# Loads of x and turned x issued from GpSimd's queue instead of SyncE's

## The reference

```
q = rotary(x @ Wq + bq)           16 heads of 32
k = rotary(x @ Wk + bk)           one head, shared by all 16
v = x @ Wv + bv                   one head, shared
attn = softmax(q k^T / sqrt(32))
x = layernorm(x + (attn v) @ Wo + bo)
W1, W2, W3 = clip(round(w / mean|w|), -1, 1)
x = layernorm(x + (sigmoid(x W1^T) * (x W2^T)) @ W3^T)      inner width 1408
```

## Time and profile before

| | us |
|---|---|
| median of 3 runs | 601.56 (600.76 to 603.36) |
| the profiled execution | 602.12 |
| its span | 600.3 |
| busy PE / DVE / ACT / POOL | 547.1 / 472.5 / 426.1 / 300.6 |
| granted share of TensorE's clock, mean | 0.971 |

### The profile page before, as it was taken

How to read it: one execution, slowest core, us unless ns; L and a number is a source line. 1 busy time by engine, 2 the same in 40 slices (tenths; PEclk the granted TensorE clock), 3 DMA queues, 4 the chain that set the end, 5 groups by cost and what they waited for, 6 DMA issues and landing times.

```text
span 600.3 us, 9190 instructions
## 1 busy us (share of the span) xinstructions
PE 547.1 (91%) x2984; PEld 273.1 (45%) x2984; DVE 472.5 (79%) x635; ACT 426.1 (71%) x865; POOL 300.6 (50%) x398
## 2 busy tenths in 40 slices
PE   9778989899788999999799999999599999989993
PEld 5444545444443444454344445354344444444441
DVE  3867878979888999899989899889989897444433
ACT  2697867779967988787878898687979796233300
POOL 2219696939589734788346325896553300201011
PEclk9789999999898999999999999999799999999997
DMA  8680428239999897999999988989899989000001
GB/s 310 190 304 17 127 50 302 55 75 195 208 193 162 151 177 150 177 198 199 220 206 185 168 162 153 183 187 197 170 208 178 169 177 192 36 1 36 1 0 70
DMA packets 217119, 92.12 MB, mean 153 GB/s; under 512 B 204400, under 2 KB 205552, under 8 KB 216560
## 3 DMA queue, kind: packets, MB, share of 16 engines
q1 hardware_dynamic: 209952, 77.61, 62.5%
q0 software_dynamic: 6144, 12.60, 10.1%
q10 hardware_dynamic: 976, 1.33, 0.6%
HBM read 20.20 MB, written 4.19 MB: 41 GB/s over the span
## 4 chain that ended last, share of the span: by engine, by line
PE 66%; DVE 10%; ACT 8%; issue 7%; POOL 4%; DMA 3%; SPq 1%; POOLq 0%; ACTq 0%; DVEq 0%
PE a_ps L1300 13%; PE b_ps L1300 7%; PE s_ps L1345 6%; PE s_ps L1313 6%; PE e_ps L1300 5%; PE c_ps L1403 5%; PE b_ps L1313 4%; PE a_ps L1231 3%; DVE p_all L1048 3%; PE c_ps L1385 3%; PE a_ps L1313 2%; ACT p_all L749 2%; PE b_ps L1285 2%; DMA pt_sb<-p_all 2%; PE s_ps L1356 2%
## 5 line engine op out<-in xcount | busy, mean ns | idle before, releaser
L749 ACT ACTIVATE p_all<-s_ps,sh_sb 128x512 f32<-128x512 f32 x192 | 130.1, 683 | 54.3 <-DVE sh_sb L1041 53.7
L1048 DVE SCALAR_TENSOR_TENSOR p_all<-p_all 128x1024 f16<-128x1024 f32 x96 | 133.0, 1385 | 4.6 <-ACT p_all L757 4.5
L1041 DVE TENSOR_REDUCE sh_sb<-s_ps 128x2 f32<-128x1024 f32 x96 | 116.5, 1214 | 17.0 <-PE s_ps L1345 17.0
L757 ACT ACTIVATE p_all<-p_all 128x1024 f16<-128x1024 f32 x96 | 101.7, 1059 | 2.0
L1300 PE MATMUL a_ps<-late,q 128*128 128x512 f16 x352 | 84.9, 385 | 4.9 <-ACT th L720 3.2
L1345 PE MATMUL s_ps<-k_st,q_st 128*128 128x512 f32 x192 | 79.1, 494 | 2.9 <-ACT p_all L749 1.6
L559 POOL TENSOR_SCALAR rstd<-mv 128x1 f32<-128x1 f32 x32 | 9.9, 308 | 136.8 <-DVE mv L1008 136.7
L430 POOL DMA_DIRECT2D q_st<-hi x96 | 49.5, 518 | 54.4 <-ACT hi L679 27.7
L1300 PEld LDWEIGHTS a_ps<-late,q 128*128 128x128 fp8e4 x352 | 32.1, 99 | 48.4 <-issue 9.3
L430 POOL DMA_DIRECT2D q_st<-lo x96 | 47.4, 498 | 9.2 <-DVE lo L951 8.7
L736 ACT ACTIVATE p_all<-s_ps,sh_sb 128x512 f32<-128x512 f32 x48 | 33.0, 693 | 21.5 <-DVE sh_sb L1035 21.5
(11 more groups left out here) (159 smaller groups left out, 1007.4 us busy)
## 6 DMA issues: line engine op xcount, KB each, us to landing
q_st<-hi POOLq DMA_DIRECT2D x96, 64.0 KB, 3.6
q_st<-lo POOLq DMA_DIRECT2D x96, 64.0 KB, 4.2
late<-in_w SPq DMA_DIRECT2D x2, 2816.0 KB, 14.1
xT_sb<-in_xT SPq DMA_DIRECT2D x8, 512.0 KB, 5.5
late<-in_x SPq DMA_DIRECT2D x4, 1024.0 KB, 6.0
out<-late SPq DMA_DIRECT2D x12, 256.0 KB, 3.2
late<-in_w SPq DMA_DIRECT2D x2, 1408.0 KB, 7.2
q_st<-hi SPq DMA_DIRECT2D x32, 64.0 KB, 2.0
```

Source lines behind the costliest of these rows:

```text
L749: act.activation(p_pair[n][:, t % 2, :], pair_banks(h * PAIRS + t // 2)[:, t % 2, :], ACT.Exp, bias=sh_sb[:, 2 * n + t % 2:2 * n + t % 2 + ...
L757: act.activation(p_half[n][:, 0, :], p_pair[n].rearrange("p t k -> p (t k)"), ACT.Copy, scale=P_SCALE).then_inc(p_hi, 1)
L1041: dve.tensor_reduce(sh_sb[:, 2 * n:2 * n + 2], pair_banks(h * PAIRS + i), AX.X, ALU.min).then_inc(maxed, 2)
L1048: dve.scalar_tensor_tensor(out=p_half[n][:, 1, :], in0=p_pair[n].rearrange("p t k -> p (t k)"), scalar=P_SCALE, in1=p_half[n][:, 0, :], op ...
```

## The change

`load_xT` for the third and fourth sequence and `load_x` for the second to the fourth move from SP's list to POOL's, with semaphores of their own. `load_xT(b + 1)` stands behind the second `inverse_std` and ahead of the stacking of head 7; `load_x(b)` stands behind the stacking of head 9 and ahead of the rotation of `q3`. The waits are those of before, and the loads of the first sequences stay on SP.

```diff
             for b in range(1, B):
                 for k in range(H * PAIRS):
-                    if k == 7 and b < B - 1:
-                        load_xT(b + 1)
                     if k:
                         turn(b, *divmod(k - 1, PAIRS))
...
-                    if k == 12:
-                        sp.wait_ge(h_ready, b * TT)
-                        load_x(b)
...
+            def load_xT(s):
+                pool.wait_ge(*filled("q3", s - 1))
+                for half in range(2):
+                    cols = slice(half * DT * T // 2, (half + 1) * DT * T // 2)
+                    pool.dma_start(xT_sb[:, :, :].rearrange("p k t -> p (k t)")[:, cols],
+                                   xT[s, :, cols]).then_inc(xT_by_pool[half], 16)
+
+            def load_x(s):
+                pool.wait_ge(h_ready, s * TT)
+                pool.dma_start(xb, x[s, :, :].rearrange("(t p) d -> p t d", p=P)).then_inc(x_by_pool, 16)
...
                 inverse_std(b - 1, 0, 0)
                 inverse_std(b - 1, 0, 1)
+                if b < B - 1:
+                    load_xT(b + 1)
                 stack(pool, b, 7)
                 inverse_std(b - 1, 0, 2)
                 inverse_std(b - 1, 0, 3)
...
                 stack(pool, b, 8)
                 stack(pool, b, 9)
+                load_x(b)
                 rotation(b, "q3")
```

More of the change, by code:

```diff
@@ L310, in layer @@
         x_in = sem("x_in")
+        xT_by_pool = [sem(f"xT_by_pool{n}") for n in range(2)]
+        x_by_pool = sem("x_by_pool")
         bo_added = sem("bo_added")
@@ L567, in inverse_std @@
                                        ALU.mult).then_inc(shift_done, 1)
+            def load_xT(s):
[7 more added lines that the diff above has]
+                pool.dma_start(xb, x[s, :, :].rearrange("(t p) d -> p t d", p=P)).then_inc(x_by_pool, 16)
             def add_bias(s, t):
-                pool.wait_ge(x_in, (s + 1) * 16)
+                if s:
+                    pool.wait_ge(x_by_pool, s * 16)
+                else:
+                    pool.wait_ge(x_in, 16)
                 pool.tensor_tensor(xb[:, t, :], xb[:, t, :], bo_sb, ALU.add).then_inc(bo_added, 1)
@@ L1228, in project_q @@
                         for half in range(2):
-                            pe.wait_ge(xT_in[half], (s + 1) * 16)
+                            if s > 1:
+                                pe.wait_ge(xT_by_pool[half], (s - 1) * 16)
+                            else:
+                                pe.wait_ge(xT_in[half], (s + 1) * 16)
                 for k in tiles:
```

## The result

The changed kernel takes 635.27 us in the median of four runs (624.75 to 639.07), the kernel before 601.16 (599.15 to 603.36); the ratio is 1.0443, 95% interval 1.0387 to 1.0499 (it is below the ratio of the medians, 1.0567, because it leaves out two slow runs of the changed kernel, over 1.5% above its fastest). The prediction was 601.1, no change. The profiled execution took 624.75, with a span of 622.9 us, 22.6 more than before.

A forecast was written before the change was run, and what follows sets the result against it. The chain of waits bounds the kernel, two thirds of it on PE. The terms 1.2 - 1.4 - 0.3 = -0.5 us on 601.56 gave 601.1 us, no measurable change, with a range of 598.3 to 605.2.

The forecast's parts named there:

- the turnings that no longer stand behind the loads: SP's list, one waited turning in body 2: freed of the load ahead, -0.3 us, 0 if equally slow beside it.
- When the turned x arrives: PE's projection in bodies 1 and 2: turned x lands 0.8 us later (0 to 2.2), hidden, cost nothing.
- The rival of the late turned x: Turned x lands 2 us later, PE idles and its clock drops: 602.8, or 604.5 with body 1; chance 0.15.
- The issue on POOL: POOL's issue of x ahead of q3's rotation and rounding in body 1: +1.2 us (0.5 to 8); turned x's issues hidden.
- The rival of the long issue: POOL pays by runs when issuing x: 603.9 at 4 us, 607.9 at 8 us; chance 0.18.
- DVE's meeting in body 2: Issuing x delays POOL's rotation, so DVE's 4.06 us lower half ends before it: -1.4 us (0 to -1.8).
- more comes back: Body 2's ctx0 regains the 2.4 GHz clock, up to 1.7 us returns: 598.7 with a short issue; chance 0.10.

The follow-up runs named there:

- the held: The changed kernel, with POOL's loads and SP's next turnings waiting so that a load and a turning are never in flight together: 616.77 us, ratio 1.0208.
- the later: The changed kernel, with POOL's issue of x moved behind the second operation of q3's rotation, some 2.5 us later: 611.10 us, ratio 1.0128.
- the quarter run: The changed kernel, with only the first 128 rows of x (256 KB, not 1 MB) loaded for sequences 1 to 3: 609.22 us, ratio 1.0111.
- the run of the meeting of DVE and POOL: The kernel before, with POOL's rotation of q3 in bodies 2 and 3 waiting for DVE's lower half of step 11: 601.05 us, ratio 0.9989.
- the benches: Four kernels of DMAs without the layer's work, turnings from SP with loads beside them; 1 MB landed in 6.2 to 8.3 us in the first.

## Why the prediction was wrong, step by step

**The step that failed** is "the turnings that no longer stand behind the loads", -0.3 us with 0 as the other end. The two ends were the turning freed of the load, and the turning as slow beside a load in another queue as behind one in its own. A turning *slower* than behind the load was not among them. Behind 1 MB in SP's list it landed in 9.9 us at worst; beside 1 MB from another queue in 20.1 and 24.5. The text said that no row showed a load beside a turning from different queues, and yet closed the range from above; the price of something unseen was bounded by the thing that it replaced. The rule of the Trainium skill weighed there ("DMA: Bandwidth & Descriptors", section "Issuing engines are not separate DMA queues") says that DMAs of all issuing engines interleave on the same 16 engines, and that another queue saves only the time to issue. The trace agrees with the first half: beside the load the turnings' packets took some 129 ns in place of 25. The second half led to the 0, and there the measurement decides against it: which queue a transfer is in changed what its neighbours paid.

From it came ACT's 23.5 us of waiting. The observation that only one turning in 96 was waited for, and for 0.3 us, was true, and was read as if turnings had no part in the time. It holds for the turnings of that trace, 9.9 us at most: in body 1 ACT came to its slot 14.6 us after the turning's issue (it had waited 9.86 when that landed at 172.17 + 24.50), in body 3 12.7 us after it, so that 20 us and more break through.

**When the turned x arrives.** The bound was 0 to 2.2 us of delay. Its second halves landed after 11.5 and 7.1 us, against 7.3 and 7.2 before: 4.2 later in body 1, and not later in body 2. In body 1 PE waits 5.5 us, and starts the projection at 159.11, which is 0.7 later than before though the body began 1.5 earlier; its eight matmuls take 6.38 us, not 5.37, at a granted clock of 0.57. The rival of the late turned x named this slowing behind a gap, and stopped at 604.5.

**A term that the sum lacked** is the longer end. POOL's closing DRAIN took 6.89 us before and 9.10 after, and the 2.2 us lie bare at the end of the span. It goes with the loads on POOL's queue: 7.96 with x alone there, 8.93 with the turned x alone, 9.1 in the held, the later and the quarter run, 9.59 with x in four loads, 8.20 with only x in quarters, and 6.89 again with the loads on ACT's queue and in the run of the meeting of DVE and POOL. No row shown ahead of the prediction has it. What the DRAIN does in that time isn't shown.

**The issue on POOL** was the right mechanism, a little less than forecast: 0.80 us for x (1.2 predicted), 0.54 to 0.64 for each half (0.8). It went onto the path at the place named, ACT's wait for the rounding growing from 4.4 to 5.2. The rival of the long issue falls; the 16-fold count of runs does not make the issue 16 times as long.

**DVE's meeting in body 2** went as forecast, though with some luck in the size. PE waits 0.21 us ahead of L1382, where it waited 1.36 ahead of the same product. The longest lower half is now

```profile
L1062 DVE SCALAR_TENSOR_TENSOR p_all<-p_all x96: 1207/1217/2765, 123.7 to 525.6; 128x1024 f16<-128x1024 f32 x96
```

where it was 4.06, and the one on the chain in body 2 takes 1.23 us (at 314.75). Body 2 is the one that gained, 1.7 us, near the -1.4, though the turning of 296.11 took 11.16 against 9.77. But another rival's term is in it too, the one called "more comes back": the product with v of the first four heads ran at full clock (granted 1.00) and took 3.6 us (from 312.22), where it took 5.3 before (from 299.31), most of it at 0.68. The low clock (0.68) now fell on the projection of `q0` instead, whose eight matmuls took 5.37 us and not 3.67 (at 303.20), a place where the prediction had it hidden, since ACT comes to its exponentials later. How much of the 1.7 is DVE's and how much the clock's isn't shown. The run of that step alone gave 1.0 in the medians, within its scatter, and in its trace the product ran in 3.6 us as well.

Not explained is the scatter of the changed kernel's runs, 14 us where the kernel before has 4: it would fit meetings that are closer in one run than in another, but only one run of it has a trace.

**What is shown and what is not.** Shown: the loss appears with either load off SP's list; ACT's queue gives slow landings as well as POOL's (there at the turned x); the slow landings of x are gone when x is issued 2.5 us later, when a quarter is loaded, or when the quarters are spread; 2.2 of the 22.6 us are POOL's closing DRAIN. Open: why 1 MB that meets a turning within 0.1 us takes 18 to 24 us in the kernel and 6 to 9 in the benches, and so what in the engines' order of packets makes it. How close the two must start is open too: at 0.34 us apart on ACT's queue they were still slow, at 1.0 us they took 10 to 13.

## What to carry to other kernels

In one queue the small urgent transfer pays for the large one ahead of it once: behind 1 MB of x a turning landed in 7.0 to 9.9 us, and the load in 5.9 to 6.8. In two queues, started at the same moment, both took some 2.5 to 3.5 times as long as that: the turning 18.1 to 24.6, the load 18.0 to 23.9. Before a load is moved off the queue of the transfers that something waits for, ask what will be in flight beside it and how many bytes; if it must move, cut it and spread the pieces over the other engine's own work. Look at the end of the span as well: loads on POOL's queue made its closing DRAIN 1.1 to 2.7 us longer. And where no row shows two things side by side, the range is open on the bad side, whatever the median of either alone.

## What the runs showed of the hardware that was not expected

- 1 MB over 512 runs of 2 KB holds POOL 0.80 to 0.82 us for the issue, 256 KB 0.54 to 0.59, a half of the turned x 0.54 to 0.64; a copy of 64 KB over 32 rows 0.50.
- Turnings issued within 0.1 us of a load from another queue took 6.4 to 9.1 us beside 256 KB, 15.6 to 18.5 beside four times 256 KB, 18.1 to 24.6 beside 1 MB; 2.5 us ahead of 1 MB, 9.0 to 11.8.
- While they crawl, the engines' busy share is full and the traffic 83 GB/s instead of 176; a turning's 256-byte packet is open for some 129 ns instead of 25 (estimates from the packets and shares of 180 to 188 and 216 to 224).
- POOL's closing DRAIN grows with the loads on its queue, from 6.89 us to between 7.96 and 9.59, and the span with it.
- 1 MB loads beside turnings, without the kernel around them, land in 6 to 9 us, with one exception of 13.4.
